# Filler products in TensorE's waits, from the end of the attention to the start of the experts

## What is computed

```python
x = x + cross_attention(layernorm(x), ctx)           # 16 heads of 8
x = x + mamba_mlp(layernorm(x))
x = x + experts(layernorm(x))                        # 8 experts, the 2 farthest centroids

# mamba_mlp(x):
x = x + mamba2(layernorm(x) * w1 + b1)
x = x + gelu(layernorm(x) @ fc_w.T + fc_b) @ proj_w.T + proj_b

# mamba2(x): one projection gives z (256), xBC (384) and dt (4 heads)
dt  = softplus(dt_raw + dt_bias)
xBC = silu(causal conv of 4 taps over the tokens)    # -> xs, B, C
h_t = exp(dt_t * A) * h_(t-1) + dt_t * xs_t * B_t ;  y_t = h_t . C_t
y   = rmsnorm((y + D * xs) * silu(z)) @ out_proj_w.T
```

## Time and profile before

| | us |
|---|---|
| median of 3 runs | 596.31 (594.64 to 597.05) |
| the profiled execution | 596.57 |
| its span, first to last instruction | 594.7 |
| mean granted TensorE clock | 0.939 of full |
| TensorE busy | 525.8 (88% of the span) |
| VectorE busy | 419.8 (71%) |
| ScalarE busy | 381.4 (64%) |

### The profile page before, as it was taken

The page is one execution under the profiler, slowest core; times in us unless marked ns, Lnnn a source line. Parts: engine busy times, 40 slices in busy tenths (PEclk is TensorE's granted clock), DMA queues, the critical chain, the costliest instruction groups (busy, mean ns, idle before and its releaser), DMA issues. The chain is left out here.

```text
span 594.7 us, 18671 instructions
## 1 busy us (share of the span) xinstructions
PE 525.8 (88%) x7814; PEld 345.1 (58%) x7814; DVE 419.8 (71%) x751; ACT 381.4 (64%) x704; POOL 323.5 (54%) x197
## 2 busy tenths in 40 slices
PE   2888999999989889999999989987697968999996
PEld 1634555565556555665566555654286645777775
DVE  5177887788778787797888779446875486555555
ACT  4873667677767667677777768863751525656562
POOL 2597877557656656558657399004000024677772
PEclk9887999999999999999999999996886878999999
DMA  7898766685594582775664591002000000000001
GB/s 210 124 132 130 161 84 104 100 124 78 87 127 73 86 117 57 112 107 85 97 87 63 95 163 49 3 2 97 1 2 1 0 1 1 2 2 0 0 0 36
DMA packets 16408, 41.61 MB, mean 70 GB/s; under 512 B 3990, under 2 KB 6814, under 8 KB 16218
## 3 DMA queue, kind: packets, MB, share of 16 engines
q1 hardware_dynamic: 15592, 40.09, 41.3%
q10 hardware_dynamic: 740, 0.42, 0.2%
HBM read 19.70 MB, written 0.52 MB: 34 GB/s over the span
## 5 line engine op out<-in xcount | busy, mean ns | idle before, releaser
L888 DVE TENSOR_REDUCE half_max<-wide 128x2 f32<-128x802 f32 x256 | 241.8, 988 | 56.3 <-PE wide L576 52.4
L814 ACT ACTIVATE probs<-score 128x512 f32<-128x512 f32 (+1 forms) x416 | 225.8, 596 | 74.0 <-PE score L627 73.6
L647 PE MATMUL sums<-probs,values 128*32 128x192 f32 (+3 forms) x3328 | 134.5, 282 | 3.7 <-issue 3.7
L647 PEld LDWEIGHTS sums<-probs,values 128*32 128x32 f32 (+1 forms) x3328 | 88.0, 110 | 57.0 <-issue 28.5
L576 PE MATMUL wide<-k_stack,q_cur 48*128 48x401 bf16 x512 | 88.2, 342 | 13.4 <-ACT k_full L796 6.1
L627 PE MATMUL score<-q_cur,k_stack 50*128 50x128 bf16 (+1 forms) x1664 | 83.5, 220 | 9.9 <-ACT probs L814 5.0
L407 POOL TENSOR_TENSOR ctx_hi<-ctx_in,one 128x1601 bf16<-128x1601 f32 x15 | 42.9, 2857 | 76.7 <-PE wide L498 67.8
L1841 POOL TENSOR_TENSOR hid_lo<-hid_e,hid_hi 114x512 bf16<-114x512 f32 x47 | 54.1, 1157 | 36.4 <-ACT hid_hi L1869 35.3
L627 PEld LDWEIGHTS score<-q_cur,k_stack 50*128 50x128 bf16 (+1 forms) x1664 | 52.4, 96 | 35.9 <-issue 12.5
L419 POOL TENSOR_TENSOR k_hi<-k_full,one 128x1601 bf16<-128x1601 f32 x15 | 42.8, 2856 | 41.7 <-ACT k_full L796 32.8
L1969 DVE SCALAR_TENSOR_TENSOR hid_e<-gu,keep_bgu,gate 114x512 f32<-114x512 f32 x48 | 35.9, 750 | 41.8 <-ACT gate L1882 40.5
(11 more groups left out here) (304 smaller groups left out, 925.8 us busy)
## 6 DMA issues: line engine op xcount, KB each, us to landing
k_stack<-k_hi SPq DMA_DIRECT2D x64, 204.0 KB, 6.4
ctx_in<-in_ctx SPq DMA_DIRECT2D x56, 200.1 KB, 6.3
k_stack<-k_lo SPq DMA_DIRECT2D x32, 204.0 KB, 8.5
ctx_in<-in_wgu SPq DMA_DIRECT2D x16, 171.0 KB, 4.7
keep_w<-in_w SPq DMA_DIRECT2D x1, 1368.0 KB
ctx_in<-in_ctx SPq DMA_DIRECT2D x1, 800.5 KB, 8.9
keep_x<-in_x SPq DMA_DIRECT2D x1, 512.0 KB, 7.0
out<-keep_x SPq DMA_DIRECT2D x2, 256.0 KB, 2.3
```

Source lines behind the costliest of these rows:

```text
L647: last = pe.matmul(sums[32 * g:32 * g + 32, first * LQ:(first + heads) * LQ], values[0:m, n, k, VW * g + 2 * c:VW * g + 2 * c + 32], probs ...
L814: nc.scalar.activation(probs[0:m, step % NPROB, :].rearrange("r (g p c) -> r p g c", g=G, p=2)[:, p], score[0:m, (2 * step + p) % NSCORE, ...
L888: dve.tensor_reduce(half_max[:, b % 2, :, u // 4, u % 4], wide[:, w, :].rearrange("p (c k) -> p c k", c=2)[:, :, 0:CH], AX.X, ALU.max).the ...
```

## The change

A function `spend` issues a number of products into a bank, each starting and stopping its own sum. At the end of the attention TensorE first waits until the ring slot of the last attention sums (`("s", 2, 0)`) is emptied and then issues nine of them into that slot, from the split context. In the middle program `idle(b, times)` issues them into bank b, from the experts' split weights, at eleven places of TensorE's list. Nobody waits for these products and nobody reads what they write; each bank is one that holds nothing wanted at that point. No other engine's list changes.

```diff
--- before.py
+++ after.py
@@ -131,6 +131,12 @@
 
 EMPTIED = {what: emptied(what) for what in ring_order()}
 HOLDERS = ring_order()
+
+
+def spend(pe, out, lhs, rhs, times):
+
+    for _ in range(times):
+        pe.matmul(out, lhs, rhs, start=True, stop=True)
 
 
 def attention(nc, A, keep):
@@ -701,6 +707,8 @@
                             project_tokens(p)
             sum_values(B - 1, NK - 2)
             sum_values(B - 1, NK - 1)
+            is_empty(pe, ("s", 2, 0))
+            spend(pe, wide[:, RING["s", 2, 0] % 2, 0:512], ctx_hi[:, 0, 0:P], ctx_hi[:, 0, P:P + 512], 9)
 
         @block.scalar
         def _(act):
@@ -1156,15 +1164,23 @@
                 pe.matmul(bank(MM_BANK[h][c]), keep.win[:, 256 + P * c:256 + P * c + P], vT[:, half(h)],
                           start=True, stop=True).then_inc(s["mm"], 1)
 
+            def idle(b, times):
+                spend(pe, bank(b), keep.w_hi[:, 0, 0, 0:P],
+                      keep.w_hi[:, 1].rearrange("p g c -> p (g c)")[:, 0:512], times)
+
             turn_last()
+            idle(0, 3)
             turn_v(0, 0, 0)
+            idle(6, 3)
             turn_tokens()
             pe.wait_ge(s["vtc"], 1)
             project_x(0, 0)
             project_tokens()
             project_x(0, 1)
             project_x(0, 2)
+            idle(1, 3)
             turn_v(0, 1, 1)
+            idle(6, 4)
             pe.wait_ge(s["vtc"], 2)
             for t in range(NT):
                 last = pe.matmul(bank(6)[:, MH * t:MH * t + MH], vT[:, tok(t)], keep.win[:, 640:644],
@@ -1178,6 +1194,7 @@
                     if c == 0:
                         pe.wait_ge(*((s["conv"], 3), (s["dts"], 2))[h])
                     elif h:
+                        idle(3, 3)
                         pe.wait_ge(s["conv"], 4)
                     pe.matmul(bank(Z_BANK[h][c]), keep.win[:, P * c:P * c + P], vT[:, half(h)],
                               start=True, stop=True).then_inc(s["zin"], 1)
@@ -1205,10 +1222,12 @@
                 last.then_inc(s["xt"], 1)
 
 
+            idle(3, 12)
             pe.wait_ge(s["dp"], 3)
             for t in range(NT):
                 last = pe.matmul(ps[0:3 * MH, 1, tok(t)], decay_parts[:, t, :], ident_bf[:], start=True, stop=True)
             last.then_inc(s["dpt"], 1)
+            idle(0, 4)
             pe.wait_ge(s["dpc"], 1)
             spread(0)
 
@@ -1290,9 +1309,12 @@
             project_out(0)
             for t in range(6, NT):
                 state(t)
+            idle(1, 6)
             project_out(1)
 
+            idle(1, 4)
             turn_v(1, 0, 0)
+            idle(2, 4)
             for h in range(2):
                 pe.wait_ge(s["vtc"], 3 + h)
                 for c in range(4):
@@ -1317,6 +1339,7 @@
                                  start=True, stop=True)
             last.then_inc(s["dots"], 1)
             turn_v(2, 1, TURN_BANK[1])
+            idle(0, 7)
 
 
         @block.scalar
```

## The result

| | before | changed |
|---|---|---|
| median of the first comparison, 4 runs each | 595.47 (591.09 to 597.05) | 588.13 (585.61 to 589.35) |
| profiled execution | 596.57 | 589.35 |
| span | 594.7 | 587.5 |
| mean granted TensorE clock | 0.939 | 0.976 |

The ratio is 0.9894, 95% interval 0.9861 to 0.9927: a small gain, clear of noise. Two later comparisons of the same two kernels gave 0.9932 (0.9904 to 0.9960) and 0.9963 (0.9931 to 0.9995).

What follows compares the result with a forecast made beforehand. Bound where VectorE or ScalarE waits for TensorE at half clock between attention and experts. 596.57 - 7.7 gained + 0.35 borders + 0.5 experts + 1.0 partial falls = 590.7, stated as 590.5; 8-in-10 range 588.3 to 594.5 us.

Steps and rivals of the forecast that it cites:

- (a): 403 to 409.6 us: VectorE waits less for TensorE's transposes before the sum into keep_x; 1.5 us gained.
- (e): 459 to 464.2 us, MLP: products ready in time for the gelus, so the fifth gelu starts earlier; 1.0 us gained.
- (c): 430 to 436.8 us: VectorE's waits for transposes behind the skip products and for first y vanish; 1.8 us gained.
- (b): 413 to 419.8 us: the 16 small dt products run faster, but VectorE waited only briefly for them; 0.5 us gained.
- (d): 450.7 to 457 us: second output projection with sums of squares at high clock, 2.8 us gained, plus 0.1 on the transposes behind.
- Borders: Ends of the attention and of the middle program: fill products end after VectorE; 0.35 us lost for both.
- Experts: Start of the experts: TensorE idles 5 us, not 2, so the clock is low when wanted at 490.84; 0.5 us lost.
- Partial falls: New unfilled TensorE waits after the last project_x and in the MLP, and 1-column products, may drop the clock; 1.0 us lost.
- the two things that the forecast had named as wrong: Clock at half from 403 on despite the fills, or real TensorE instructions delayed past their releasers by running fills.
- R1: Rival: clock holds in part, falling at about 450 anyway; 592.4 us and up, 593.8 with one more fall; chance 0.2.
- R3: Rival: TensorE is faster but VectorE and ScalarE are ready no sooner; 594.5 us; chance 0.08.
- R2: Rival: fills don't move the clock and overrun at low clock on the chain; 4.2 us slower, 600.5; chance 0.05.

Runs made afterwards that it cites:

- experiments 2 and 3: The changed kernel with only its first three groups of products, 591.74 us; and without the groups of 6, 4 and 4 around the second output projection, 591.70 us.
- experiment 1: The changed kernel with all 62 products passing 4 columns in f32 instead of 512 in bf16, for nearly the same time: 596.95 us, ratio to before 1.0051.
- experiment 6: The changed kernel with every group of products twice as long (124 products): 597.57 us, ratio to before 1.0060.

## Why the prediction was right, and where its sizes were off

The time forecast, 590.5, was 5.8 under the median then known; the medians of the three comparisons lie 7.3, 3.8 and 3.5 apart (6.3, 4.0 and 2.2 by the ratios). The side and the mechanism hold. The size is on the high side of the mean: on the ledger 5.85 was forecast and 4.3 came over three profiles each. Some of the fit to the first pair is luck: it compares with a slow execution of the kernel before, the one that I had read the terms from.

*(a) and (e)* came as priced, in every profile: 1.5; 1.3 for 1.1 with the transposes' 0.1. *(c)* came as 1.9 for 1.8 in the two executions without a fall there and as 0.3 in the third. *(b)* is 0.6 for 0.5 against the first profile of the kernel before and nothing against the other two, in which the step is as short as in the changed kernel (8.3 us from keep_x to dt_x).

*(d)* was the term most mis-sized, and its cause is the least shown. In the pair of profiles it is 2.7 for 2.8, over three profiles 2.3. I took one execution of the kernel before for the kernel: from first y to the second rms the three profiles of the kernel before take 15.9, 14.8 and 15.9 us against 13.2 in the changed one, and the two kernels without products there (experiments 2 and 3) take 13.2 as well, as does the one with four-column products. So the gain is there, but it came without the products placed there too, and what those are worth stays open between 0 and 2.7 us. An execution of 596.57 was also near the slow end of what the kernel before spreads over (587.0 to 597.05 in all comparisons), and I took it for the base.

*Borders*: 0.35 charged for both, 0.3 measured in two of three executions: nothing at the first (TensorE's products end at 399.68, and VectorE is idle for 0.66 us before its memset, as before), 0.3 at the second, and 1.45 there in the execution where the group ran low. That last case I had only in the rival.

*Experts*: 0.5 charged, 0.3 to 0.45 measured against the first profile and 0.9 against the mean of three, by the mechanism named: 4.90 us of waiting, then the first nine of the products at 0.43. It came in all three profiles of the changed kernel.

*Partial falls*: 1.0 charged; 0.8 in every execution and another 1.55 in one of three. The fall after the last project_x came as foreseen (2.68 us idle, clock low at 419). I wrote that it would cost little, since VectorE is ahead there; it cost 0.84, because the group of twelve, fitted to a wait of 2.9 us, began later behind the slow z products and ended after decay_parts was ready. That is one of the two things that the forecast had named as wrong: I had costed the fills in the middle program at nothing, their wait as their cover. The one before vT's second half (1.49 us idle) and the one near 450 came in none of the changed kernel's three profiles; one at the skip products, which I had not named, came in one. Of the products' own price the traces settle the one open question: 12 took 2.75 us from the first start to the last end and 22 took 4.91, 0.22 each. The 131 ns of the Trainium skill ("TensorE: Matmul & The Clock Gate", section "Back-to-back issue gap") is not seen in any run.

R1 (the clock holds in part) is what the execution of 594.3 was, by other places. R3 (VectorE ready no sooner) is ruled out by the waits of VectorE that went; its price did not follow from its own terms either, since (a) and (d) halved are 2.15 us, which gives 594.2 and not 594.5. R2 (the groups run low and overrun) is what experiment 1 made; experiment 6 overran at the high clock.

## What to carry to other kernels

Price a low clock only where another engine waits for TensorE inside it; then take a second and third profile before believing the sum, since the low stretches move from one execution to the next. Products of 512 columns in bf16 held the clock in these waits, products of 4 columns in f32 did not. They must be fewer than the wait holds even when TensorE arrives late or low, and a wait left empty can push the next filled one over its end.

## What I had not expected of the hardware

Being busy did not keep the clock: 9.30 of 9.6 us busy with four-column products and small ones, at half clock. The same kernel's low stretches began at 403, 413, 430 and 450.7 in one execution and at 399.8, 413.5, 427 and 447.5 in another. And the start of the middle program, before which nothing differs but nine products, lay anywhere between 397.2 and 402.2 us in the profiles of all kernels but the doubled one, a spread of 5.0 us, more than the whole change is worth (4.3); what moves it was not looked for.
